# Expert layers of a hybrid model kernel: block numbers read into registers without range checks, eight ahead of the scatters; ranking, scores and the next layer's normalisation placed earlier

## The reference

```
logits = hidden @ router_w.T                       # 16 experts
top_vals, top_idx = jax.lax.top_k(logits, 1)       # one expert a token
scores = sigmoid(top value)                        # scales the token's row
gate, up = split(score * hidden @ gate_up_proj[e])
routed = (up * silu(gate)) @ down_proj[e]
shared = silu(hidden @ shared_gate_w.T) * (hidden @ shared_up_w.T) @ shared_down_w.T
x = x + shared + routed
```

## Time and profile before

| | |
|---|---|
| median of 3 runs | 710.61 us (706.87 to 721.05) |
| profiled execution | 705.19 us, its span 703.9 us |
| instructions | 7562 |
| busy, share of the span | TensorE 79%, VectorE 67%, ScalarE 44%, GpSimd 42% |
| HBM | 32.97 MB read, 26.02 MB written |

### The profile page before, as it was taken

One profiled execution on the slowest core, in us unless ns is written; L12 is line 12 of the kernel. 1 busy time (PEld: TensorE's weight loads), 2 busy tenths in 40 slices (PEclk: granted clock), 3 DMA queues, 4 the chain that ended last, 5 costly groups with the idle time before them and its releaser, 6 DMA issues.

```text
span 703.9 us, 7562 instructions
## 1 busy us (share of the span) xinstructions
PE 553.6 (79%) x2162; PEld 300.5 (43%) x2162; DVE 471.5 (67%) x904; ACT 311.6 (44%) x591; POOL 298.4 (42%) x264
## 2 busy tenths in 40 slices
PE   2968999999555989788398878869877885819897
PEld 1624556566334755623032233324323422517655
DVE  5299693785221335596699999999999995303334
ACT  2752525243211532477755556545654651205321
POOL 0066331352320026000677786679769765200071
PEclk9987865899675999898589989989998999859999
DMA  8999400000003321000000000000000000014212
GB/s 329 393 316 332 157 0 1 1 15 16 16 15 93 91 61 50 0 1 0 0 0 1 1 0 0 1 15 0 1 0 15 1 0 15 16 44 118 68 49 75
DMA packets 22392, 40.67 MB, mean 58 GB/s; under 512 B 3280, under 2 KB 19152, under 8 KB 21456
## 3 DMA queue, kind: packets, MB, share of 16 engines
q1 hardware_dynamic: 20016, 34.63, 14.8%
q0 software_dynamic: 2048, 4.20, 2.1%
q10 hardware_dynamic: 288, 1.37, 0.6%
HBM read 32.97 MB, written 26.02 MB: 84 GB/s over the span
## 4 chain that ended last, share of the span: by engine, by line
DVE 29%; PE 26%; issue 13%; SPq 5%; ACT 5%; POOL 1%; DMA 1%; DVEq 0%; ACTq 0%; POOLq 0%
DVE arena L1219 14%; PE psum L617 6%; DVE psum L1213 6%; PE psum L668 5%; SPq L1671 4%; PE psum L627 3%; DVE arena L1166 2%; PE psum L689 2%; PE psum L790 2%; DVE stats L858 1%; PE psum L656 1%; PE psum L679 1%; PE psum L385 1%; SPq L1675 1%; ACT xn L1298 1%
## 5 line engine op out<-in xcount | busy, mean ns | idle before, releaser
L1644 POOL TENSOR_TENSOR arena<-arena 128x512 f32<-128x512 f32 x128 | 159.4, 1268 | 59.8 <-DVE arena L1219 59.7
L790 PE MATMUL psum<-arena,w 128*128 128x512 f32 x256 | 138.0, 642 | 15.6 <-DVE arena L1231 10.3
L1219 DVE TENSOR_TENSOR_SCAN arena<-arena,psum 128x512 f32<-128x512 f32 x128 | 148.5, 1201 | 0.0
L1510 ACT ACTIVATE arena<-arena 128x510 f32<-128x510 f32 x128 | 89.9, 717 | 63.5 <-DVE arena L1219 59.2
L1608 POOL DMA_INDIRECT arena<-by_expert,routes x32 | 30.7, 959 | 128.0 <-DMA by_expert<-arena 118.8
L1213 DVE TENSOR_TENSOR psum<-psum,arena 128x512 f32<-128x512 f32 x128 | 81.6, 682 | 3.8 <-PE psum L775 3.8
L775 PE MATMUL psum<-arena,c 96*128 96x512 bf16 x128 | 48.9, 412 | 40.7 <-DVE arena L1219 29.9
L790 PEld LDWEIGHTS psum<-arena,w 128*128 128x128 f32 x256 | 46.8, 200 | 72.2 <-POOL arena L1644 42.9
L617 PE MATMUL psum<-xnt,w 128*128 128x512 f32 x128 | 65.0, 659 | 5.0 <-ACT arena L1410 3.2
L1116 DVE TENSOR_TENSOR arena<-psum,arena 128x256 f32<-128x256 f32 (+1 forms) x32 | 13.3, 416 | 73.1 <-ACT arena L1430 73.1
L1563 POOL TENSOR_TENSOR arena<-arena 128x512 f32<-128x512 f32 x16 | 20.3, 1272 | 96.6 <-DVE arena L919 96.6
(11 more groups left out here) (181 smaller groups left out, 967.5 us busy)
## 6 DMA issues: line engine op xcount, KB each, us to landing
by_expert<-w_in SPq DMA_DIRECT2D x4, 4096.0 KB, 45.4
w<-w_in SPq DMA_DIRECT2D x1, 4431.5 KB, 13.3
arena<-by_expert SPq DMA_DIRECT2D x62, 64.0 KB, 1.9
by_expert<-arena SPq DMA_DIRECT2D x62, 64.0 KB, 1.6
by_expert<-w_in SPq DMA_DIRECT2D x1, 1984.0 KB, 70.6
x<-x_in SPq DMA_DIRECT2D x4, 256.0 KB, 7.5
c<-c_in SPq DMA_DIRECT2D x1, 1024.0 KB, 15.4
out<-x SPq DMA_DIRECT2D x4, 256.0 KB, 2.2
```

What stands on the lines that cost most here:

```text
L790: nc.tensor.matmul(bank(6 + c), ident, state[c][s % 3], start=(n == 0), stop=(n == DS - 1)).then_inc(*summed.inc((s, c)))
L1219: nc.vector.tensor_tensor_scan(state[c][s % 3], decay_b[c][s % 2], bank(2 * c + s % 2), 0.0, ALU.mult, ALU.add).then_inc(*state_ready.inc( ...
L1510: nc.scalar.activation(live, seq, ACT.Exp, scale=a_neg[:, DS * c + n:DS * c + n + 1]).then_inc(*decay_ready.inc((s, c)))
L1644: nc.gpsimd.tensor_tensor(state[c][s % 3], state[c][s % 3], c_row[s % 3], ALU.mult).then_inc(*y_done.inc((s, c)))
```

## The change

1. `register(...)`, a new helper, reads a number into a register with the bounds stated for the compiler and without the run-time check. SyncE uses it for block numbers, TensorE for expert numbers.
2. SyncE reads eight block numbers (`KNOWN`) ahead of its wait for the scatters, and one more behind each fetch until all 31 are read.
3. `rank` has no work put in its middle any more: the shared chunk `project(0, 1)` moves from before the last ranking's wait for one-hot rows to after the whole ranking. This holds for both turns.
4. In turn 0, ScalarE's `score_of(1, 2)` moves from after the last group's `take_turned` to directly after `exp_of_score(1, 2)`.
5. For the selective scan, groups 0 and 1 are scaled by VectorE ahead of `add_shared(2)`; TensorE transposes them, projects u of group 0, then transposes groups 2 and 3; ScalarE's order follows, with the silu table after the last `take_turned`.

```diff
+KNOWN = 8
+        def register(engine, place, below):
+            return nc.values_load(place, engines=(engine,), min_val=0, max_val=below - 1,
+                                  skip_runtime_bounds_check_because="the slots of all experts are fewer than the blocks")
...
-            def rank(n, g, ring, meanwhile=None):
+            def rank(n, g, ring):
...
-                if meanwhile:
-                    meanwhile()
...
-                pending(lambda: project(0, 0), lambda: project(0, 1))
+                pending(lambda: project(0, 0))
...
-                        chosen_expert[s] = nc.tensor.value_load(expert_int[s:s + 1, 0:1], min_val=0, max_val=NE - 1)
+                        chosen_expert[s] = register(mybir.EngineType.PE, expert_int[s:s + 1, 0:1], NE)
...
     TensorE, selective_scan:
-                for g in GROUPS:
+                for g in range(2):
                     turn(2, g, ring)
...
                 project_u(0)
+                for g in range(2, NGRP):
+                    turn(2, g, ring)
...
     VectorE, experts, last groups:
+                    if t == 0 and g == NGRP - 1:
+                        for of in range(2):
+                            scale(2, of)
                     if g > EARLY:
                         add_shared(g - 1)
...
-                for g in GROUPS:
+                for g in range(2, NGRP):
                     scale(2, g)
...
     ScalarE, selective_scan:
-                for g in GROUPS:
+                for g in range(2):
                     root(2, g)
-                table_set(SILU)
-                for g in GROUPS:
+                for g in range(2):
                     take_turned(2, g)
...
+                for g in range(2, NGRP):
+                    root(2, g)
                 project_u(0)
+                for g in range(2, NGRP):
+                    take_turned(2, g)
+                table_set(SILU)
...
     ScalarE, pending_a:
                 exp_of_score(1, NGRP - 2)
+                score_of(1, NGRP - 2)
                 root_rms(BATCH - 1)
...
                 take_turned(1, NGRP - 1)
-                score_of(1, NGRP - 2)
                 exp_of_score(1, NGRP - 1)
...
     SyncE:
-                block = [nc.sync.value_load(block_int[s:s + 1, 0:1], min_val=0, max_val=N_BLOCKS - 1) for s in range(NSLOT)]
-                place = [by_expert[bass.ds(b * P, P), :] for b in block]
+                place = {}
+
+                def find(s):
+                    at = register(mybir.EngineType.SP, block_int[s:s + 1, 0:1], N_BLOCKS)
+                    place[s] = by_expert[bass.ds(at * P, P), :]
+
+                for s in range(KNOWN):
+                    find(s)
                 sp.wait_ge(*scatter[t][NBLK - 1])
                 for s in range(NSLOT):
                     nc.sync.dma_start(xs_rows[:, s, :], place[s]).then_inc(*fetch[t][s // GB * GB].inc(s))
+                    if s + KNOWN < NSLOT:
+                        find(s + KNOWN)
```

More of the change, by code:

```diff
@@ L629, in down @@
                     r.then_inc(*down_made.inc((t, g)))
-                pending(lambda: project(0, 0), lambda: project(0, 1))
+                pending(lambda: project(0, 0))
                 for g in range(EARLY):
                     for c in range(NSC):
-                        if (g, c) not in ((0, 0), (0, 1)):
+                        if (g, c) != (0, 0):
                             project(g, c)
@@ L820, in selective_scan, with pending @@
                 last_ring = Ring([bank(4), bank(5)], [c_ready[last], placed[3, NGRP - 2]])
-                def pending(project, project_next):
+                def pending(project):
                     project()
@@ L826, in pending @@
                     logits_of(3, NGRP - 1, last_ring)
-                    rank(3, NGRP - 1, last_ring, project_next)
+                    rank(3, NGRP - 1, last_ring)
                 rings = [Ring([bank(i), bank(i + 1)], [state_ready[n_steps - 2, i // 2], state_ready[n_steps - 1, i // 2]]) for i in (0, 2)]
@@ L840, in pending @@
                 logits_of(1, NGRP - 1, others)
-                rank(1, NGRP - 1, others, project_next)
+                rank(1, NGRP - 1, others)
             u0 = n_units
```

## The result

The changed kernel takes **669.03 us** (median of 4 runs, 668.59 to 677.48) against 708.74 (4 runs, 706.01 to 721.05) for the kernel before beside it: ratio **0.944, 95% interval 0.940 to 0.949**. The forecast was 665.7 with a range of 656 to 678. The execution that was traced took 677.48, its span is 676.2. One thing has to be known to read all times here: executions reach the scoring of the first layer up to 14 us apart (between 153.1 and 167.6 us in the 14 traces, by a mean granted TensorE clock of 0.92 down to 0.75 between 60 and 150 us), although nothing ahead of it was changed, so I count stretches of two traces from that point. It is ScalarE's activation that finishes the scores of the second group: 167.62 us in the trace of before (L1317), 165.07 in this one (L1326).

A forecast was written before the change was run, and what follows sets the result against it. The bound was SyncE's 31 serial checked block-number reads, behind which the experts waited each turn. Savings of 16.9, 14.3, 6.4, 2.0 and 5.3 us sum to 44.9, giving 660.3 for the profiled execution, 665.7 as median, range 656 to 678.

The forecast's parts named there:

- SyncE's reads: SyncE's queue before the fetches: unchecked loads 0.31 us instead of 0.58, eight ahead; fetches with a load 0.85 apart.
- the scatters as the gate: Before SyncE's fetches: the unmoved wait for scatters becomes the limit; first turn, eight loads end 1.3 us before it.
- (a): SyncE's register loads: removing checks removes nothing, 0.58 us a load stays; 678 us; chance 0.12.
- (c): SyncE's fetches: a load behind a DMA issue waits for its landing, 2.3 us a fetch; +15, 726 us; chance 0.04.
- Scores and rank sooner: First turn, ScalarE's scores and TensorE's ranking: block numbers 4.6 us sooner, last sends from 190.0 instead of 194.6.
- rival (b): TensorE's shared chunk behind the ranking, clock low: TensorE ready 4 to 6 us after the fetches; 676 us; chance 0.08.
- TensorE's loads: TensorE's slot loop: without checks on expert numbers, 0.5 us saved a quad, 3.2 a turn, 6.4 us together.
- Clock: TensorE's first quad after the shortened pause: may stay at 2.4 GHz instead of 1.2; 1 us a turn, 2.0 together.
- Normalisation: Hand-over to next layer: groups 0 and 1 scaled early, first convolution at 294.1 instead of 299.43, 5.3 us sooner.
- the cover for ScalarE's table load: Next layer's first convolution: hides the silu table load with 0.5 to 1 us left; otherwise 0.2 to 1 lost.
- The sum: Whole kernel: 16.9 + 14.3 + 6.4 + 2.0 + 5.3 = 44.9 us saved, profiled execution 705.19 to 660.3.
- The level of the median: Whole kernel: the profiled execution was 5.4 us below the median of three runs, so 660.3 becomes 665.7 as median.

The follow-up runs named there:

- e7: Kernel before with only TensorE's loads of expert numbers made without range checks; 683.63 us, ratio 0.990.
- e10: Changed kernel with twelve block numbers read ahead of the scatters instead of eight; 649.31 us, ratio 0.937 to the kernel before.
- e8: Changed kernel with GpSimd's gathers of the last two groups held until TensorE's second shared down projection; 650.65 us, ratio 0.940 to the kernel before.
- e6: Kernel before with only the next layer's normalisation of groups 0 and 1 moved earlier and the table change behind it; 690.54 us.
- e1: Changed kernel run again without edit on the first chip of the experiments; 669.26 us, ratio 0.940 to the kernel before.
- e9: Changed kernel without edit, run as control on the third chip; 649.66 us, ratio 0.936 to the kernel before.
- the last version: Changed kernel, first eight fetches without loads between, first pair's products before the next transposes, last two groups' gathers held; 643.95 us, ratio 0.907 to the kernel before.

## Why the prediction was right

Stretches of two traces that both lack the late burst, the kernel before and the control run of the changed kernel, each from the starts named (us). The forecasts of the first and the fifth are for the start of the experts, which moved by -17.0 (from 54.1 to 37.1 after the scoring) and, in the second turn, by -13.8.

| stretch | before | changed | difference | forecast |
|---|---|---|---|---|
| scoring to the first transposes, first turn | 50.8 | 33.5 | -17.2 | -16.9 |
| first transposes to first shared chunk behind the slots | 38.1 | 34.3 | -3.8 | -3.2 and -1 of clock |
| from there to the last landing addition | 33.5 | 33.5 | 0 | 0 |
| to the first convolution | 9.5 | 4.0 | -5.5 | -5.3 |
| to the first transposes, second turn | 330.7 | 316.2 | -14.5 | -14.3 |
| slots, second turn | 37.2 | 34.7 | -2.6 | -3.2 and -1 of clock |
| to the end | 36.6 | 35.2 | -1.4 | 0 |
| scoring to the end | 536.3 | 491.4 | **-44.9** | **-44.9** |

- **SyncE's reads: right.** Load 0.31 apart, fetches 0.82 (forecast 0.85), the scatters as the gate: the last is sent at 191.40 and lands 2.2 later, at 193.6, and the first fetch is at 193.80, with the loads (from 189.7) over. The forecast took the price of a load between two DMA issues from TensorE's loads; it held. Rivals (a) and (c), a period of 0.58 of its own and a wait for the transfer, are both out by the 0.82. The floor of some 600 ns which the Trainium skill gives a `tensor_load` ("DMA: Bandwidth & Descriptors", section "Latency and other measured facts") is not there: 0.31 from load to load, and 0.27 for the load itself, on this chip.
- **Scores and rank sooner: right,** 4.5 us to the last send in the traces (30.9 to 26.3 after the scoring), as worked out. Alone, the order is worth 0.987.
- **TensorE late, rival (b): no.** Its first transposes begin at 198.59 in the changed kernel, behind 0.78 us of waiting for VectorE's shared addition, and it is 2.08 us ahead of the second four.
- **TensorE's loads: right in sum, the term built of wrong pieces.** A quad fell from 4.06 to 3.70, not to 3.5, which is 2.3 over 6.5 quads; most of the rest of the 3.1 measured a turn (e7) is in the drain, which the forecast had left out.
- **Clock: right in one turn, and only in some executions.** Windows of the loop's first 8 us in the kernel before and in the control, then behind the wait for the eighth slot in e10, whose TensorE code is the control's:

```profile
218.40:226.40 8.00, 6.86 (x22) 5.05 (x23) 0.92 (x3) 1.96 (x4) 0.00 (x0) 0.50 0.46 125
```
```profile
198.70:206.70 8.00, 5.71 (x30) 3.83 (x31) 1.18 (x3) 2.76 (x6) 0.00 (x0) 1.00 0.27 75
```
```profile
193.30:197.30 4.00, 3.97 (x13) 3.12 (x14) 0.46 (x2) 1.33 (x3) 0.00 (x0) 0.57 0.25 69
582.50:586.50 4.00, 4.00 (x15) 3.16 (x15) 0.85 (x3) 1.13 (x3) 0.00 (x0) 0.57 0.28 80
```

In the control the clock stays up through the first turn's wait, in e10 it falls behind it in both turns (e8 likewise). From the start of the experts to the loops' end the two turns together gain 7.2 us in the control, 5.8 in e8 and 5.3 in e10, of which the loads alone make 5.9 (e7). So the clock gave between 0 and 1.3 us, not 2.0.
- **The 1.4 at the end is not the change's.** The clock is 0.65 in the four us behind the second loop of the kernel before and 1.00 in the control, but also 1.00 in e6 and e7, which leave that place as it was, and 0.67 in e10, which has the whole change:

```profile
667.30:671.30 4.00, 4.00 (x8) 1.74 (x7) 0.66 (x1) 0.87 (x2) 0.99 (x1) 0.65 0.17 49
```
```profile
621.40:625.40 4.00, 4.00 (x12) 1.85 (x11) 1.04 (x2) 1.47 (x3) 0.00 (x0) 1.00 0.20 53
```

- **Normalisation: right,** and with it the cover for ScalarE's table load.
- **The sum: that 44.9 meets 44.9 is in part luck.** It holds for this pair of traces, with the 1.4 of the end in it. From the scoring to the end e8 and e10 take 493.1 and 494.5 us, the control 491.4. The medians, side by side on one chip, differ by 39.7 (the result), 40.5 (e1), 40.5 (e8) and 44.0 (e9). The reads, the order and the normalisation hold everywhere; what the forecast has too much is mostly in the loops, where it counted on 8.4 with the clock. An estimate for the rest: e6 and e7, with their own parts added back (528.1 + 5.5, 527.9 + 6.2), put the kernel before at some 534 us from the scoring on rather than 536.3, since they lack the 1.4 at the end; 534 less 493.1 to 494.5 is 40 to 41, which is what most medians show.
- **The level of the median: a step that was off.** "It was faster than all three runs, whose median is 5.4 above; so 665.7 as a median" treats the gap as scatter that carries over. It mixes two things. The traced execution had a late start of the layers and no late burst; runs at 706 to 711 have, by their level, the reverse. Like for like, the control's traced execution took 657.89 with its scoring at 165.20, 2.4 us before that of the kernel before; 657.9 + 2.4 = 660.3, which is the sum's number. As a median the forecast was 3.3 us low beside executions that have the burst, and 15 to 16 high beside those of the second and third chip, which don't; the ratio is the same on both. So the measured median came close to the forecast with a wait in it that the forecast didn't know and a comparison of levels that was wrong; only the difference between the kernels is a test of it.

## What to carry to other kernels

An in-order queue that reads addresses and then waits should read only as many as the wait hides. A read put between two transfers costs its full period (0.82 us from fetch to fetch against 0.53), so put the reads behind the transfers that somebody waits for: starting the first eight fetches at once, with one small reordering, took 1.5 to 2.2 us off each loop against the control, 0.9 to 1.3 of it beyond the reordering, while a larger lead alone took off nothing.

A level that differs by chip can hide in a comparison of one traced execution with a median. Before a new wait is blamed on the change, trace both kernels on one chip, and the changed one on a second; here four traces of one chip had the wait and all seven of two others had none.

## What the runs showed of the hardware

**Late completion signals.** In the first trace of the changed kernel and in all four of the first chip, TensorE's signals came 8 to 9.4 us late in one burst, in both turns, while GpSimd issued 16 indirect gathers 1.25 us apart. Signals up to 246.9, with nine gathers issued, came in time; the next, due at 250.5 behind the twelfth, did not. They were let go 3.8 us after the start of the last gather. On the second and third chip there was no delay, with the same gathers at the same relative times. With the last eight gathers put behind the signal it didn't occur on the fourth, where the kernel before runs at the higher level. Shown is the delay in the traces, its tie to the chip, and its absence there with the gathers held. That the kernel before has the wait at its 706 to 711 us, and that the row of gathers is what holds the signals, is argued from the times (18 us apart for the kernel before, 19 for the changed one, 64 us and not 45 for the last version): no traced execution of the kernel before fell on such a chip, and in the last kernel two other edits went along, though neither touches these stretches. One more number speaks for the first: without the wait the kernel before takes 536.3 us from the scoring on, so its 709.76 and 708.03 would put the scoring at 172 and 170 us, and no trace has it later than 167.6. Why the chips differ stays open.

**A load between two fetches.** From fetch to fetch it takes 0.53 us without a load, 0.82 with an unchecked and 1.10 with a checked one. With the checks back on both engines the first turn's loop is 7.2 us longer (41.8 against 34.6): 2.0 of it is the longer wait for the eighth slot, 3.1 what TensorE's checks are worth alone (e7), and the other 2.1 was not measured by itself; the clock of 0.50 behind that wait is the likely cause.
